# Two-layer graph attention: late adjacency tiles, one eviction per projection, the eighth query tile from PSUM

## The reference

```python
h = relu(layernorm(x))
q, k, v = (h @ W.T + b for each of q, k, v)              # 4 heads of 64
scores = clip(q . k / 8, -10, 10); scores[adj == 0] = -10
attn = softmax(scores over each chunk of 256 keys)
out = layernorm((sum over chunks of attn @ v) @ Wo.T + bo + h) * gamma + beta
x = x + out
h = relu(layernorm(x))
q = h @ W                                                # 4 heads of 64
e = leaky_relu(q . a_src (row) + q . a_dst (column), 0.2); e[adj == 0] = -9e15
x = x + elu(softmax(e) @ q)
```

## Time and profile before

| | |
|---|---|
| median of three runs | 4141.56 us (4134.57 to 4146.01) |
| profiled execution | 4135.93 us, span 4134.1 us |
| busy share of the span | TensorE 94%, VectorE 85%, ScalarE 67%, GpSimd 59% |
| first layer | up to about 2,780 us |
| granted TensorE clock, mean | 0.99 |

### The profile page before, as it was taken

The page is one execution under the profiler, slowest core; times in us unless marked ns, Lnnn a source line. Parts: engine busy times, 40 slices in busy tenths (PEclk is TensorE's granted clock), DMA queues, the critical chain, the costliest instruction groups (busy, mean ns, idle before and its releaser), DMA issues. The chain is left out here.

```text
span 4134.1 us, 167624 instructions
## 1 busy us (share of the span) xinstructions
PE 3882.4 (94%) x72712; PEld 3228.9 (78%) x72712; DVE 3513.9 (85%) x5974; ACT 2779.1 (67%) x3088; POOL 2440.7 (59%) x1893
## 2 busy tenths in 40 slices
PE   7999999999999999999999999979898998999988
PEld 5877777777777787777777777758888888888887
DVE  5888888788788788888878878869999999999899
ACT  5655555555555555555555556539899998998987
POOL 4453455345354355345534534339988989889897
PEclk9999999999999999999999999989999999999999
DMA  6110110111011011011011100111213122132121
GB/s 133 30 28 22 33 33 23 33 28 33 28 28 28 23 38 28 20 36 33 23 33 28 33 22 26 43 39 45 82 41 90 52 70 87 35 91 68 49 77 39
DMA packets 170002, 178.77 MB, mean 43 GB/s; under 512 B 7184, under 2 KB 157072, under 8 KB 169104
## 3 DMA queue, kind: packets, MB, share of 16 engines
q1 hardware_dynamic: 166144, 156.08, 13.2%
q0 software_dynamic: 3088, 11.54, 1.3%
HBM read 107.02 MB, written 34.62 MB: 34 GB/s over the span
## 5 line engine op out<-in xcount | busy, mean ns | idle before, releaser
L829 ACT ACTIVATE slot<-slot,shift 128x1024 f32<-128x1024 f32 x1024 | 1077.2, 1085 | 933.0 <-PE slot L675 931.8
L514 POOL TENSOR_TENSOR ctx_sum<-ctx_sum,parts 128x256 f32<-128x256 f32 x896 | 651.0, 735 | 1327.3 <-DVE parts L989 1326.9
L968 DVE SCALAR_TENSOR_TENSOR probs<-slot,bound 128x1024 f32<-128x1024 f32 x1024 | 1243.6, 1218 | 95.8 <-ACT slot L829 89.0
L687 PEld LDWEIGHTS outs<-v_s,probs 128*64 128x64 f32 x32768 | 1007.5, 137 | 243.8 <-issue 166.1
L687 PE MATMUL outs<-v_s,probs 128*64 128x66 f32 x32768 | 1090.9, 223 | 43.0 <-DVE parts L989 30.8
L1723 DVE SCALAR_TENSOR_TENSOR p_dve<-t_ps,b_small,mask 128x1024 f32<-128x1024 f32 x832 | 1045.4, 1277 | 89.3 <-ACT t_ps L1613 78.7
L1613 ACT ACTIVATE t_ps<-s_all,d_rel 128x1024 f32<-128x1024 f32 x832 | 917.5, 1116 | 107.8 <-DVE p_dve L1723 94.2
L674 PE MATMUL slot<-q_hl,k_hl 128*128 128x512 f32 x2048 | 883.5, 431 | 28.5 <-DVE probs L968 20.4
L675 PE MATMUL slot<-q_hl,k_hl 128*128 128x512 f32 x2048 | 806.0, 394 | 0.0
L1442 POOL TENSOR_SCALAR p_pool<-r_all,b_big,b_small 128x1024 f32<-128x1024 f32 x192 | 726.2, 3782 | 43.6 <-ACT r_all L1605 31.4
L674 PEld LDWEIGHTS slot<-q_hl,k_hl 128*128 128x128 f32 x2048 | 384.7, 188 | 149.9 <-DVE probs L968 38.8
(11 more groups left out here) (150 smaller groups left out, 3939.2 us busy)
## 6 DMA issues: line engine op xcount, KB each, us to landing
q_hl<-q_hl SPq DMA_DIRECT2D x128, 256.0 KB, 3.6
s_all<-s_turned SPq DMA_DIRECT2D x64, 512.0 KB, 5.5
x_q_s<-in_x SPq DMA_DIRECT2D x32, 512.0 KB, 4.6
x<-y SPq DMA_DIRECT2D x32, 512.0 KB, 3.1
t_o_s<-x SPq DMA_DIRECT2D x16, 1024.0 KB, 5.3
out<-t_o_s SPq DMA_DIRECT2D x16, 1024.0 KB, 7.9
x_q_s<-x SPq DMA_DIRECT2D x28, 512.0 KB, 7.1
probs<-in_adj POOLq DMA_DIRECT2D x12, 512.0 KB, 7.1
```

The costliest lines, as they stand in the source:

```text
L514: nc.gpsimd.tensor_tensor(ctx_sum[:, :, h, :], ctx_sum[:, :, h, :], parts[:, adds_before(i) % PARTS, :, :], ALU.add).then_inc(ctx_added, 1)
L687: end = nc.tensor.matmul(outs[i % OUTS][rows_of, q, 0:V_COLS], probs[:, i % PROBS, r, q * P + g * D:q * P + (g + 1) * D], v_s[:, c * JC + ...
L829: nc.scalar.activation(slot[:, :, :], slot[:, :, :], ACT.Exp, bias=shift[:, 0:1], scale=SCALE).then_inc(act_done, 1)
L968: nc.vector.scalar_tensor_tensor(probs[:, i % PROBS, :, :], spot(kind, "step", s, i)[:, :, :], P_LOW, bound[:, c % 2, :, :], ALU.max, ALU. ...
```

## The change

1. Only the first four adjacency tiles are turned in the prologue. The other twelve are turned inside strip 0 of the first batch, after steps 5, 7, ... 27. Each takes a use of the slot ring; its sixteen blocks fill one slot and ScalarE takes the Sign of all 2,048 columns in one operation. VectorE frees the slot with a memset of one element, in front of the next step's clip. The loads use a ring of three buffers (`ctx_t`, `y` and one new one); three are issued in the prologue and nine by GpSimd within the strip. The three stores of the mask for GpSimd's tiles wait for all tiles.
2. Second layer: the weights' columns, and so the projection's, stand head by head, 64 features and then the two dot products; a row of the target is a one and these 66 columns. `keep_q` is one operation of 264 columns. `sd` is used for batch 0 only.
3. Second layer: `tail` and its copy go. At j = 2 VectorE inverts the eighth tile's sum and the seven others from PSUM (`invert_tail`, `invert`), at j = 3 it scales the eighth tile from PSUM (`keep_tail`), at j = 4 the seven. `DEFER` is 4 and `RING` 7.

```diff
+ADJ_FIRST = STRIP // P
+ADJ_LATE = NT - ADJ_FIRST
+LATE_RING = 3
+MASK_AT = tuple(5 + 2 * n for n in range(ADJ_LATE))
...
+            if first and s == 0 and i in MASK_AT:
+                use("m", MASK_AT.index(i))
...
                     if first and s == 0:
+                        sp.wait_ge(mask_written, ADJ_PARTS * ADJ_FIRST + ADJ_LATE)
                         for k, j in enumerate(POOL_AT):
                             sp.dma_start(mask_dram[:, k, :], mask8[:, j, :]).then_inc(mask_stored, 16)
...
+            def load_late(n):
+                if n >= LATE_RING:
+                    pool.wait_ge(slot_filled, used(0, FIRST, "m", n - LATE_RING) + 1)
+                m = ADJ_FIRST + n
+                pool.dma_start(adj_late[n % LATE_RING], adj[m * P:(m + 1) * P, :]).then_inc(late_loaded[n % LATE_RING], 16)
...
+                        if first and s == 0 and i + 2 in MASK_AT[:ADJ_LATE - LATE_RING]:
+                            load_late(MASK_AT.index(i + 2) + LATE_RING)
                         if chunk_and_head(i)[0] > 0:
                             add_part(b, s, i)
...
+            def late_mask_tile(n, use, slot):
+                pe.wait_ge(late_loaded[n % LATE_RING], (n // LATE_RING + 1) * 16)
+                fill(use)
+                turned = slot[:, :, :].rearrange("p r n -> p (r n)").bitcast(F16).rearrange("p (t n) -> p t n", n=P)
+                for jt in range(NT):
+                    last = nc.tensor.transpose(turned[:, jt, :], adj_late[n % LATE_RING][:, jt * P:(jt + 1) * P], ident16)
+                last.then_inc(slot_filled, 1)
...
-            for n, (s, hp) in enumerate(k_order()):
+            for s, hp in k_order():
                 keys(s, hp, t_first(2 * s + 1), k_first(s, hp), slots[k_first(s, hp) % SLOTS])
-                mask_tile(4 + n)
...
+            def late_mask_tile(n, use, slot):
+                act.wait_ge(slot_filled, use + 1)
+                m = ADJ_FIRST + n
+                turned = slot[:, :, :].rearrange("p r n -> p (r n)").bitcast(F16).rearrange("p (t n) -> p t n", n=P)
+                nc.scalar.activation(mask8[:, :, m * P:(m + 1) * P], turned, ACT.Sign).then_inc(mask_written, 1)
...
+            def late_mask_kept(n):
+                dve.wait_ge(mask_written, ADJ_PARTS * ADJ_FIRST + n + 1)
+                nc.vector.memset(dve_cell[:, 0:1], 0.0).then_inc(slot_free, 1)
...
+                        if first and s == 0 and i - 1 in MASK_AT:
+                            late_mask_kept(MASK_AT.index(i - 1))
                         if i < STEPS:
                             clip(s, i)
...
-RING = 6
+RING = 7
-DEFER = 3
+DEFER = 4
...
-                for side, q in enumerate((near, far)):
-                    nc.scalar.activation(q[pb % 2][:, tile, 0:2 * E1].rearrange("p (h e) -> p h e", e=E1)[:, :, 0:D],
-                                         pro[:, side * 2 * D:(side + 1) * 2 * D].rearrange("p (h d) -> p h d", d=D),
-                                         ACT.Identity, bias=zero[:, 0:1], scale=rstd[:, k % 2, t:t + 1])
-                nc.scalar.activation(sd[:, :, tile, :], pro[:, F:WIDE].rearrange("p (s h) -> p s h", s=2),
+                nc.scalar.activation(q_all[pb % 2][:, tile, :, 1:Q_H], pro[:, 0:WIDE].rearrange("p (h e) -> p h e", e=H_W),
                                      ACT.Identity, bias=zero[:, 0:1], scale=rstd[:, k % 2, t:t + 1]).then_inc(pro_free, 1)
...
+            def invert_tail(b, m):
+                f = b * UNITS + m
+                dve.wait_ge(p_used, RING + (f + 1) * ND)
+                first = m % HALVES * V_COLS
+                nc.vector.reciprocal(rc[:, MAIN:HT], sums[:, HALVES, first:first + 1]).then_inc(tail_rc_done, 1)
+
             def keep_tail(b, m):
                 f = b * UNITS + m
-                dve.wait_ge(p_used, RING + (f + 1) * ND)
-                nc.vector.tensor_copy(tail[:, :], sums[:, HALVES, m % HALVES * V_COLS:(m % HALVES + 1) * V_COLS])\
+                dve.wait_ge(tail_rc_done, f + 1)
+                first = m % HALVES * V_COLS + 1
+                nc.vector.tensor_scalar(v[:, MAIN, :], sums[:, HALVES, first:first + D], rc[:, MAIN:HT], None, ALU.mult)\
                     .then_inc(tail_kept, 1)
...
-                nc.vector.tensor_scalar(v[:, MAIN, :], tail[:, 0:D], rc[:, MAIN:HT], None, ALU.mult).then_inc(v_done, 1)
...
                             if j == 2:
+                                invert_tail(*prev)
+                                invert(*prev)
+                            if j == 3:
                                 keep_tail(*prev)
```

More of the change, by code:

```diff
@@ L126, in k_order, with count_uses @@
     return [(s, hp) for s in range(NS) for hp in range(H // 2)]
-def count_uses(last):
+def count_uses(last, first=False):
     place = {}
@@ L138, in count_uses @@
             use("step", s, i)
-            if i == TURN_AT:
+            if i == TURN_AT and not (first and s == 0):
                 use("turn", s)
-            if i == W_AT:
+            if i == W_AT and not (first and s == 0):
                 use("project", s)
+            if first and s == 0 and i in MASK_AT:
+                use("m", MASK_AT.index(i))
             if i in t_pairs(s) and not last:
@@ L313, in used @@
             place = USES[kind][name]
-            skipped = 2
             if kind == FIRST:
-                skipped = sum(place >= USES[kind][(gone, 0)] for gone in ("turn", "project"))
-            return b * BATCH_USES + PROLOGUE_USES - skipped + place
+                return PROLOGUE_USES + place
+            return b * BATCH_USES + PROLOGUE_USES + FIRST_USES - BATCH_USES + place
         def spot(kind, *name):
@@ L702, in batch @@
                             values(s, i - LAG)
+                        if first and s == 0 and i in MASK_AT:
+                            n = MASK_AT.index(i)
+                            late_mask_tile(n, used(b, kind, "m", n), spot(kind, "m", n))
                         if i == TURN_AT and has_before:
@@ L823, in batch @@
             def batch(b, kind):
-                last = kind == LAST
+                first, last = kind == FIRST, kind == LAST
                 for s in range(NS):
@@ L1253, in layer1_block @@
         h_t = sb("h1_t", [P, KC, STRIP])
[L1255 to L1257 removed]
+        near_0 = both.x_s[:, 0:NT * Q_W].rearrange("p (t e) -> p t e", t=NT)
+        far_0 = both.h_s[:, 0:NT * Q_W].rearrange("p (t e) -> p t e", t=NT)
+        q_all = [sb(f"q_all{k}", [P, NT, H, Q_H]) for k in range(2)]
         sd = both.sd
@@ L1416, in _ @@
                                     base=0, pattern=[[-1, P]], channel_multiplier=1).then_inc(consts_ready, 1)
-            for q in (near[1], far[1]):
-                nc.gpsimd.memset(q[:, :, D:D + 1], 1.0)
-                nc.gpsimd.memset(q[:, :, E1 + D:Q_W], 1.0).then_inc(ones_ready, 1)
+            for q in q_all:
+                nc.gpsimd.memset(q[:, :, :, 0], 1.0).then_inc(ones_ready, 1)
             pool.wait_ge(ones_ready, 2)
```

107 lines of the change are left out of this document (51 added, 56 removed).

## The result

The changed kernel takes 4113.36 us in the median of four runs (4109.09 to 4118.22); the kernel before, timed beside it, 4140.72 (4134.57 to 4146.01, four runs). Between the two profiled executions the difference is smaller, 4134.1 against 4116.4 us of span, 17.7 us; the profiled run after was the slowest of its four.

The account below looks back on a forecast made before the run. TensorE was taken to bound strip 0, three nearly equal engines the second layer. Terms -16.8 + 14.0 - 11.4 - 8.6 = -22.8 us, off the 4141.6 median, gave 4119 us; range 4100 to 4137.

Parts of the forecast that it names:

- Prologue, -16.8: Prologue: with twelve mask tiles gone, the first scores come at 70.7 us instead of 87.5, saving 16.8 us.
- Strip 0, +14.0: First batch's strip 0: twelve tiles' transposes on a gapless TensorE, 1.09 us each plus about 0.08 for a semaphore, cost 14.0 us.
- Rival (c): Prologue: gives nothing if adjacency loads hold up the start, so the kernel takes 4136 us; chance 0.08.
- near tie of the slot ring: Strip 0: waiting for a freed slot takes 6.2 us, TensorE's own work meanwhile 6.1, with a wait here and there.
- The step that failed: Strip 0: VectorE gets only a one-element memset per late tile, though it waits there for the eviction.
- the two terms: Mask part: the prologue's -16.8 us and strip 0's +14.0 us.
- Evictions, -11.4: Second layer: one eviction per projected tile instead of three saves 0.44 us, 26 times on the chain, 11.4 us.
- chain's 26 pieces: Second layer: the `sd` eviction stands 26 times on the chain of waits, three or four tiles a batch.
- Rival (b): Second layer: the evictions give nothing as TensorE is as full, so the kernel takes 4130 us; chance 0.14.
- Rival (a): Second layer: freed ScalarE lets VectorE run ahead in a batch's last units, 10 us more, 4109 us; chance 0.20.
- Tail, -8.6: Second layer: scaling the eighth tile from PSUM saves 8.6 us over 23 operations on the chain, 3.7 in the last batch.
- near -7: Second layer's tail: the term if scaling from PSUM loses its double rate, a few hundredths of a microsecond a unit.

Follow-up runs that it names:

- e5: The changed kernel with nine sixteenths of each late mask tile's Sign done once more on ScalarE in strip 0; 0.9975 of the kernel before.
- e11: The kernel before plus only twelve one-element memsets on VectorE in the first batch's strip 0; 1.0015 of the kernel before.
- e1: The kernel before with the mask part alone, keeping the old layout, ring and scaling; 0.9999 of the kernel before.
- e12: e9 with two late mask tiles back in the prologue and 118 idle memsets at the start of VectorE's stream; 0.9882 of the kernel before, 4088.09 us.
- e13: Like e12 but with 246 idle memsets, putting VectorE's loop code 256 instructions further on than before; 0.9875 of the kernel before, 4087.16 us.
- e2: The kernel before with the single-operation evictions and their column layout alone; 0.9963 of the kernel before.
- e3: The kernel before with the tail part alone: eighth tile scaled from PSUM, RING 7, DEFER 4; 0.9986 of the kernel before.
- e6: The kernel before with the eighth tile scaled from PSUM alone, RING 6 and DEFER 3 kept; 0.9988 of the kernel before.
- e7: The kernel before with RING 7 and DEFER 4 alone; 0.9999 of the kernel before.
- e9: The changed kernel without ScalarE's second-layer 'x1 - 1', and with two strip loads issued one batch earlier; 0.9901 of the kernel before.

## Why the prediction held, and where its sum was off

**Prologue, -16.8.** Measured -17.8: 16.9 by the shorter loops, as the middle batch's rows had it, and 0.9 by an earlier start. Rival (c) is out.

**Strip 0, +14.0.** Measured +12.5. The 0.08 us a tile for a semaphore was not there. The near tie of the slot ring did not cost anything, but it is real: the prediction had 6.2 us against 6.1, and e5 found some 0.3 us a tile to spare.

**The step that failed** is the one that costs VectorE's twelve one-element memsets at nothing ("VectorE gets only a one-element memset"), and with it the silent assumption that the loop behind them stays as it is. They cost the mask part its gain: 3.5 us between strips 3 and 27 in the kernel after, 3.7 in e11, where they are the only change. e1, the mask part alone, is 0 (within 4 us) where the two terms say -2.8 and its own first strip -4.3; the timing of e1 would not exclude -2.8, but its trace shows the lead gone by the last store of the first layer (2777.2 against 2776.8). That the code's place in VectorE's stream sets this, and that 128 instructions bring it back, is shown by e11, e12 and e13. The last section ties the late places to the transfers of VectorE's code; what holds the engine there is not seen. Between strip 27 and the last store another 1.8 us went; that is within what this stretch differs by from kernel to kernel (-1.2 to +3.0), and I leave it open.

**Evictions, -11.4.** The second layers of the profiles give -11.0 (e2), the timing -15 (9.9 to 21). That the first is so near is luck: places 2 to 7 lost 15.8 us, and 4.8 came back at places 1 and 8, where units scatter in every kernel. So the term was some 4 us too small. The cost of one operation was right, 565 ns against 560 by my line through two sizes, and the saving lies near where I put it: 1.3 us at place 2, 0.6 at place 5, 0.4 at place 6. But 0.44 us for each of the chain's 26 pieces makes 0.9 for the third unit, which is too little, and why it gained more is open. Rival (b) is out. Rival (a) put 10 us more at the end of a batch, at a tile of 1.4 us; place 7 shows nothing of it in e2 (19.2 as before), nor does place 8 without a stall (19.8 as before). The Trainium skill, ScalarE: Activation LUTs, section What ACT_TABLE_LOAD costs, gave an estimate of 0.59 us for that operation; the trace agrees within 5% (0.565).

**Tail, -8.6.** Measured -6 (2 to 10) by e3 and -5 (1 to 9) by e6. The last batch gave 4.8 where I had 3.7. The other batches gave 0.1 us at place 7 and 0.3 to 0.5 at boundaries without a stall, 3 to 4 us at most, where I had 4.9; e3's stalls at boundaries took more than that, so that its second layer is only 2.7 us shorter, e6's 4.1. Of the chain's 17 pieces outside the last batch 13 are of the sixth and seventh units, where the old scaling took 0.24 to 0.39 us: I took each piece off whole, though the new one stands in its place. The long ones of the fifth units, 1.6 to 1.8 us, are not on the chain, and place 5 stayed at 21.5. The new scaling takes 0.274 us, 0.05 above my estimate. The direction of VectorE: DVE Perf Modes in the Trainium skill, section Why PSUM operands drop a tier, agrees: 274 ns from PSUM against 240 from SBUF undisturbed. My figure of near -7 by that section charges a few hundredths to all 64 units; on the 23 pieces of the term it would be near -8. Ring and deferral cost nothing and give nothing (e7), as predicted.

**Sum.** By the profiles -17.8 + 12.5 + 5.6 - 18.3 = -18.0 against 17.7 measured between the spans, where 5.6 is what the first layer lost after strip 0 (0.3 up to strip 3, 3.5 up to strip 27, 1.8 to the last store); I had -22.8. By the medians it was -27, and the forecast of 4119 lies between the two. The runs with one part each give about 0, -15 and -6 where I had -2.8, -11.4 and -8.6. So the order of the three parts held, and that the sum came out within 5.6 us is in part luck: the mask part and the tail gave less than forecast, the evictions more. The lower end of the range, 4100, is a few us below what its two terms give (4109 less 5.4).

## What to carry to other kernels

In a loop bound by TensorE, time an edit ahead of the loop by the loop too: compare two equal stretches of it before and after, and the number of waits of each kind in them. A few instructions more on an engine cost each later pass 0.6 us here, and idle ones brought it back; try that last, since every edit undoes it. An operation that waits till one of another engine has ended has no fixed price: take it from the rows where it is alone and where it is not. Count only what is on the chain at a place where no other engine is full, and take off the difference between old and new, not the whole of the old one. Compare single units, not only sums: a few stalls can hide or feign a gain.

## What the hardware did that I had not expected

**Code has a position.** e12's memsets at VectorE's start, timeline:

```profile
1.86 3.54 DVE L917 MEMSET v_s<- 128x4176 f32 x1 [1.86 <-issue]
5.35 1.03 DVE L921 MEMSET pads<- 128x1 uint8 x58
6.78 1.73 DVE L921 MEMSET pads<- 128x1 uint8 x60 [0.39 <-issue]
```

58 memsets run without a break, 18 ns apart; then nothing happens for 0.39 us with no wait in the code. The break stands before the 64th instruction of VectorE's stream, as the trace counts them. The profile of the kernel after has two queues of instructions, here from strip 3 to 27 (packets, MB, share):

```profile
q8 instruction: 249, 4.08, 0.8%
q14 instruction: 120, 0.98, 0.2%
```

16 KB a packet on one, 8 KB on the other. Nine of the 8 KB packets of a pass move with VectorE's code. In the kernel before they start when VectorE is at instruction 94, 219, 348, 482, 604, 732, 855, 987 and 1,112 of the 1,130 of a pass (operations and waits together), in the second pass; in e11, with twelve instructions more ahead of the loop, at 80, 212, 335, 464, 587, 723, 849, 980 and 1,102; in e12 they are back within one of those of before. They stand 122 to 136 instructions apart. Late operations stand beside them: in all six passes such a packet starts 0.65 to 0.96 us after number 226 in the kernel before, and 0.66 to 0.93 us after 461 in e11. Of e11's six late operations 99, 341, 397 and 461 have such a packet within 1 us in every pass; 172 and 234 wait for an exponent of ScalarE. So VectorE's code comes in pieces of 8 KB, about 128 instructions, and the engine is late about where one piece ends. Whether it waits for the piece or for the order to fetch the next, the trace does not say; and at most of the nine places the delay hides behind other waits.

The Trainium skill, Runtime: NRT & Kernel Launch, section Instruction fetch mechanics, has engines refill their code in blocks of 16 KiB, 256 instructions, with the cost of a boundary mostly hidden. By that block e13 would be restored and e12 not; both were, with the same late places, so here the pattern repeats at 128 instructions, 8 KB, and what is not hidden costs 0.6 us a batch.

**TensorE stands still beside full transfers.** In the kernel after, at a batch's boundary, TensorE stops three times with no releaser:

```profile
3130.42 3.92 PE L1543 MATMUL sums<-q_all,p_dve 128*64 128x66 f32 x74 [2.03 <-issue]
...
3141.20 0.51 PE L1543 MATMUL sums<-q_all,p_pool 128*64 128x66 f32 x10 [1.50 <-issue]
...
3147.41 0.51 PE L1543 MATMUL sums<-q_all,p_pool 128*64 128x66 f32 x10 [2.26 <-issue]
```

The windows just before and just after the first stop (the last three columns are granted clock, DMA share, GB/s):

```profile
3126.00:3130.00 4.00, 1.94 (x51) 1.58 (x48) 4.00 (x8) 3.45 (x4) 3.92 (x3) 1.00 1.00 348
3130.50:3134.00 3.50, 3.50 (x73) 3.50 (x74) 3.50 (x5) 3.50 (x5) 3.42 (x2) 0.56 0.46 162
```

The DMA engines are full at 348 GB/s when it stops, and in the 3.5 us after the stop of 2.03 us the granted clock is 0.56, close to the lower of the two levels, 1.2 GHz of 2.4. This unit lasts 23.0 us instead of 19.3. e9 moved two loads and longer units came up where they went, which ties the stalls to the transfers. What is held up is TensorE's own code, by all that the trace shows: a 16 KB packet of instructions starts at 3127.98, 3138.68 and 3145.24 us, 2.2 to 2.5 us before each stop ends. From 2,830 us on the kernel after has 28 stops of TensorE of over 1 us without a releaser, and every one ends 2.2 to 2.8 us after such a packet starts; the packets themselves take about 1 us, and 254 of them come in 1,290 us.
